# Small norm and routing arithmetic moved into PSUM banks, in a selective-scan mixer with a low-rank feed-forward layer

## The chip, the cores and the metric

The kernel runs on one core of one Trainium2 chip. The metric is the device time of one execution in microseconds. The engines are named as in the profile: PE is TensorE (PEld its weight loads), DVE is VectorE, ACT is ScalarE, POOL is GpSimd, SP is SyncE, which issues the DMAs.

## The reference, cut to what matters

There are four sequences of 512 tokens with 1024 features. Each goes through a mixer and a feed-forward layer, each followed by an addition and a layer norm.

```python
# mixer, D = 2048 channels, N = 16 states, R = 64
u, z = split(W_in @ x);  u = silu(causal_conv4(u) + conv_b)
dt, B, C = split(Wx @ u)                      # 64, 16, 16 rows
dt, B, C = rmsnorm(dt), rmsnorm(B), rmsnorm(C)  # eps 1e-6
delta = softplus(Wdt @ dt + dt_bias)
h_t = exp(delta_t * A) * h_{t-1} + delta_t * u_t * B_t
y_t = sum_n C_t[n] * h_t[n] + D * u_t
x1 = layernorm(x + W_out @ (y * silu(z)))     # eps 1e-5
# feed-forward: ranks 8, 16, 32, 64, the best one for each token
p = softmax(gate_w @ x1 + gate_b);  keep ranks up to the argmax, weight 1
out = layernorm(x1 + W @ x1 + b + B @ (mask * (A @ x1)))
```

## The kernel before, in words

The heart is the scan. For each of 4 sequences, 4 groups of 4 channel tiles and 16 states there is a unit, 256 in all. POOL forms the unit's input (`drive`, L1311, 128x2048), ACT forms four `decay` tiles in PSUM (L1146), DVE runs four scans (L913), PE transposes the states into two banks (`turn`, L771), and the products with C are added up in `y_acc`, either by DVE alone (`add`, L921) or by ACT and POOL (`scale` L1166, `sum` L1316). Everything else runs beside it: the products of the input projection for the next sequence (L798 to L800, three matmuls of split precision for each step), convolution and gates, the output projection (L821), the feed-forward products, the norms and the routing of the sequence before.

The order of each engine's work is fixed before launch. `Plan.arrange` simulates the five engines with a cost in microseconds and a due time for each piece (`put(engine, due, us, stage, key, needs, take, give, spare)`), and each engine then runs its list strictly in that order, waiting on semaphores. Pieces also take and give back buffers from pools: three PSUM banks (`bank`), four scratch tiles, four raw and four split weight slots. A product takes a bank only if another is free (`spare=1`). Five more banks hold the decays and the turned states.

The stages that the change touches:

- `ssm_mm`: dt, B and C for 4x128 tokens into one bank (96 columns each; the bank state_t0 for the first sequence). `ssm_copy` (ACT, L1210) copies it to `narrow` in SBUF and gives the bank back.
- `ssm_stat` (DVE): squares (L1037), three sums (L1042), three times scale and add epsilon (L1046). `ssm_sqrt` (ACT, L1213). `ssm_dt` (DVE, L1050, L1054): reciprocal, dt normalized, twice, into a scratch tile. `ssm_norm` (L1059, L1062, L1065): C and B normalized. `ssm_turn_dt` and `ssm_turn_b` (PE) transpose them. Then come delta, softplus, `du` and the drives of the next sequence.
- `route_rows` (PE) transposes the low-rank products and scores into a bank; `route_copy` (ACT, L1270) copies it to `narrow`. `route_max` (DVE, L1069, L1073, L1076), `route_exp` (ACT, L1280), `route_pick` (DVE, L1081 to L1103), `route_mask` (DVE, L1115), then `route_turn` (PE), `lora_cols`, `lora_low` and the products `f_lora`.
- Layer norms: statistics (L996, L1001) on DVE, `ln1_var` or `ln2_var` (DVE, L1009) adds epsilon, root on ACT (L1254), `ln_shift` (DVE, L1012, L1015), then `rows` are normalized on ACT (L1248), some in the last sequence on DVE (L1020).

## Time and profile before

| | |
|---|---|
| median of 3 runs | 2390.41 us (2381.63 to 2395.63) |
| profiled execution, its span | 2390.45 us, 2388.7 us |
| busy share PE, DVE, POOL, ACT | 89%, 87%, 75%, 63% |
| mean granted TensorE clock | 0.942 |
| chain that ended last, by engine | DVE 37%, PE 36%, issue 11%, ACT 6%, POOL 3% |
| one table load on ACT (L1146) | 1283 ns |

Busy time counts an instruction from its start to its end, whatever it does in between. The median of the runs and the profiled execution agree to 0.1 us; 1.75 us of the latter lie outside the span.

### The profile page before, as it was taken

Reading aid. Unit: us, or ns where it says so; the run is one execution under the profiler, and the core shown is the slowest. Engines: PE = TensorE matmul, PEld = TensorE weight load, DVE = VectorE, ACT = ScalarE, POOL = GpSimd, SP = SyncE. Lnnn points to the kernel's source line nnn. Section 1 sums busy time; section 2 is a strip of 40 time slices with the busy share of each in tenths; the row PEclk is TensorE's granted clock in tenths of the full one; section 3 lists DMA queues with packets and bytes.
Section 4 is the critical chain, followed back from the end, with each engine's and each line's share of the span. In section 5 each row is a group of like instructions: output and inputs, shape, how many; then the busy total and the mean of one; then the engine's idle time right before and its main releaser. Section 6 shows DMA issues by size and latency. Waiting matters only on the chain.

```text
span 2388.7 us, 30714 instructions
## 1 busy us (share of the span) xinstructions
PE 2124.3 (89%) x10528; PEld 1582.9 (66%) x10528; DVE 2084.7 (87%) x2464; ACT 1495.8 (63%) x2133; POOL 1803.3 (75%) x769
## 2 busy tenths in 40 slices
PE   8998679788879978889989998989989999898987
PEld 6767567676655547678866556767875567675556
DVE  4458899999999999989989998999979998999732
ACT  4388677776666575566667667575576568665421
POOL 4378888899699987868768996787768987688500
PEclk9989889899889989989989999999999999998998
DMA  4366566455323334566444334465453336353313
GB/s 149 131 220 216 183 208 201 162 199 174 99 73 91 111 116 152 180 219 202 151 151 125 112 95 144 139 239 170 148 184 104 108 100 208 102 168 117 85 50 132
DMA packets 152652, 353.53 MB, mean 148 GB/s; under 512 B 17776, under 2 KB 27376, under 8 KB 152496
## 3 DMA queue, kind: packets, MB, share of 16 engines
q1 hardware_dynamic: 152496, 351.56, 45.8%
q8 instruction: 84, 1.38, 0.2%
q14 instruction: 72, 0.59, 0.1%
HBM read 282.65 MB, written 68.85 MB: 147 GB/s over the span
## 4 chain that ended last, share of the span: by engine, by line
DVE 37%; PE 36%; issue 11%; ACT 6%; POOL 3%; DVEq 0%; ACTq 0%; POOLq 0%
DVE drive L913 20%; PE state_t L771 10%; DVE y_acc L921 9%; PE bank L821 7%; PE bank L798 5%; PE bank L799 5%; PE bank L800 5%; DVE scratch L928 2%; POOL drive L1311 2%; ACT decay L1146 1%; DVE ln_stats L996 1%; ACT L1146 1%; PE bank L771 1%; PE bank L866 1%; DVE rows L983 1%
## 5 line engine op out<-in xcount | busy, mean ns | idle before, releaser
L1311 POOL TENSOR_TENSOR drive<-delta_u,b_bcast 128x2048 f32<-128x2048 f32 x256 | 1171.3, 4577 | 142.9 <-PE state_t L771 140.6
L913 DVE TENSOR_TENSOR_SCAN drive<-decay,drive 128x512 f32<-128x512 f32 x1024 | 1193.2, 1203 | 74.3 <-ACT decay L1146 51.6
L1146 ACT ACTIVATE decay<-delta,a_sb 128x512 f32<-128x512 f32 x1024 | 693.6, 688 | 395.1 <-DVE drive L913 390.7
L771 PE MATMUL state_t<-identity,drive 128*128 128x128 f32 x4096 | 614.8, 291 | 183.5 <-DVE drive L913 138.2
L771 PEld LDWEIGHTS state_t<-identity,drive 128*128 128x128 f32 x4096 | 507.9, 149 | 394.0 <-DVE drive L913 197.7
L798 PE MATMUL bank<-cols_high,w_split 128*128 128x512 f32 (+1 forms) x1280 | 550.1, 430 | 15.9 <-POOL w_split L1336 8.4
L921 DVE SCALAR_TENSOR_TENSOR y_acc<-state_t,c_rows,y_acc 128x512 f32<-128x512 f32 x711 | 505.4, 734 | 51.4 <-PE state_t L771 49.6
L800 PE MATMUL bank<-cols_high,w_split 128*128 128x512 f32 (+1 forms) x1280 | 513.5, 401 | 0.0
L799 PE MATMUL bank<-cols_low,w_split 128*128 128x512 f32 (+1 forms) x1280 | 513.1, 401 | 0.0
L821 PE MATMUL bank<-channels,w_raw 128*128 128x512 f32 x960 | 452.3, 595 | 0.0
L1316 POOL TENSOR_TENSOR y_acc<-y_acc,scaled 128x512 f32<-128x512 f32 x249 | 320.4, 1287 | 170.7 <-ACT scaled L1166 167.6
L798 PEld LDWEIGHTS bank<-cols_high,w_split 128*128 128x128 f32 (+1 forms) x1280 | 248.7, 194 | 61.9 <-issue 10.7
L800 PEld LDWEIGHTS bank<-cols_high,w_split 128*128 128x128 f32 (+1 forms) x1280 | 246.7, 193 | 58.2 <-issue 0.2
L799 PEld LDWEIGHTS bank<-cols_low,w_split 128*128 128x128 f32 (+1 forms) x1280 | 248.9, 194 | 40.6 <-issue 0.5
L821 PEld LDWEIGHTS bank<-channels,w_raw 128*128 128x128 f32 x960 | 166.0, 192 | 122.7 <-issue 121.1
L1166 ACT ACTIVATE scaled<-state_t,c_rows 128x512 f32<-128x512 f32 x249 | 170.1, 683 | 117.8 <-PE state_t L771 91.3
L1336 POOL TENSOR_TENSOR w_split<-w_raw,w_split 128x512 fp32r<-128x512 f32 (+1 forms) x114 | 145.9, 1288 | 84.1 <-ACT w_split L1186 84.0
L928 DVE SCALAR_TENSOR_TENSOR scratch<-bank,conv_w_sb,scratch 128x511 f32<-128x511 f32 (+2 forms) x192 | 142.6, 743 | 36.9 <-ACT scratch L1192 32.4
L1146 ACT ACT_TABLE_LOAD x91 | 116.8, 1283 | 1.6
L1325 POOL TENSOR_TENSOR delta_u<-delta,channels 128x512 f32<-128x512 f32 x64 | 80.6, 1286 | 35.3 <-ACT delta L1235 15.4
L1201 ACT ACT_TABLE_LOAD x63 | 80.8, 1283 | 40.6 <-PE bank L800 39.7
L1332 POOL TENSOR_TENSOR channels<-channels,scratch 128x512 f32<-128x512 f32 x64 | 82.5, 1305 | 24.0 <-DVE channels L973 20.8
(152 smaller groups left out, 1397.6 us busy)
## 6 DMA issues: line engine op xcount, KB each, us to landing
w_split<-w_split SPq DMA_DIRECT2D x288, 512.0 KB, 3.6
b_bcast<-b_rows SPq DMA_DIRECT2D x256, 256.0 KB, 3.4
w_raw<-in_w_out SPq DMA_DIRECT2D x128, 256.0 KB, 2.9
w_raw<-in_w_in SPq DMA_DIRECT2D x96, 256.0 KB, 4.1
gates<-scratch SPq DMA_DIRECT2D x64, 256.0 KB, 3.8
scratch<-gates SPq DMA_DIRECT2D x64, 256.0 KB, 4.5
rows<-in_x_rows SPq DMA_DIRECT2D x4, 2048.0 KB, 9.5
out<-rows SPq DMA_DIRECT2D x16, 512.0 KB, 5.1
```

The costliest lines, as they stand in the source:

```text
L771: last = engine.transpose(bank[0:tile.shape[1], i * P:(i + 1) * P], tile, identity[:, :])
L798: engine.matmul(bank[:, :], high[:, k % WK, :], cols_high[:, k, :], start=first, stop=False)
L799: engine.matmul(bank[:, :], high[:, k % WK, :], cols_low[:, k, :], start=False, stop=False)
L800: engine.matmul(bank[:, :], low[:, k % WK, :], cols_high[:, k, :], start=False, stop=last).then_inc(signal[stage])
L821: engine.matmul(bank[:, :], tile[:, k % WK, :], chan[s % 2][:, k, :], start=(k == tiles[0]), stop=(k == tiles[-1])).then_inc(signal["o_mm"])
L913: engine.tensor_tensor_scan(state, decay[(GT * s + t) % DECAYS][:, :], state, 0.0, ALU.mult, ALU.add).then_inc(signal["scan"])
L921: engine.scalar_tensor_tensor(y_acc[:, tt, :], bank[:, :], c, y_acc[:, tt, :], ALU.mult, ALU.add).then_inc(signal["add"])
L928: m = engine.scalar_tensor_tensor(conv[:, back:T], bank[:, 0:T - back], conv_w[:, j, KC - 1 - back:KC - back], conv[:, back:T], ALU.mult, ...
L1146: engine.activation(decay[i % DECAYS][:, :], delta[:, g % 2, t, :], ACT.Exp, scale=a_sb[:, j, n:n + 1]).then_inc(signal["decay"])
L1166: engine.activation(scaled[:, :], bank[:, :], ACT.Copy, scale=c_rows[b % 2][:, tt, n:n + 1]).then_inc(signal["scale"])
L1311: engine.tensor_tensor(drive[key % DRIVES][:, :, :], du[:, :, :], row, ALU.mult).then_inc(signal["drive"])
L1316: engine.tensor_tensor(y_acc[:, tt, :], y_acc[:, tt, :], scaled[:, :], ALU.add).then_inc(signal["sum"])
```

## The change: what it does

- `narrow`, `score` and `prob` in SBUF go. dt, B, C and the normalized C before its weight stay in the bank of `ssm_mm`; low-rank rows, scores, probabilities and an inverse stay in the bank of `route_rows`. B normalized goes to a small SBUF tile `b_narrow`. Of the two tensors that a DVE instruction reads there, at most one now lies in SBUF.
- `ssm_copy` and `route_copy` go. Squares are formed on ACT out of the bank (`ssm_square`). Scale and epsilon of the mixer's norms, and epsilon of the layer norms, become scale and bias of the root on ACT; the bias is an SBUF column set once at the start. `ssm_sqrt` is two instructions. `ln1_var` and `ln2_var` go, their waits move to `ln1_sqrt` and `ln2_sqrt`.
- The bank of `ssm_mm` is given back after `ssm_norm` in place of `ssm_copy`, that of `route_rows` after `route_mask` in place of `route_copy`. The first `turn` waits for `ssm_norm`.
- The costs given to the planner are smaller: `ssm_stat` 2.2 to 0.7, `ssm_dt` 1.2 to 0.9, `ssm_norm` 1.0 to 0.5, `route_max` 1.6 to 0.6, `route_pick` 3.5 to 2.2, `route_mask` 2.4 to 1.3. So the order of all work is computed anew.

```diff
-        put("ACT", due + 0.4, 0.5, "ssm_copy", b, [...], give=[("bank", ("ssm_mm", b))] if b else [])
-        put("DVE", due + 0.5, 2.2, "ssm_stat", b, [("ssm_copy", b)], take=[("scratch", ("twice", b))])
+        put("ACT", due + 0.4, 0.5, "ssm_square", b, [("ssm_mm", (b, TT - 1))], take=[("scratch", ("twice", b))])
+        put("DVE", due + 0.5, 0.7, "ssm_stat", b, [("ssm_square", b)])
...
+        put("DVE", due + 0.7, 0.5, "ssm_norm", b, [("ssm_dt", b)] + ([("ssm_turn_b", b - 1)] if b else []),
+            give=[("bank", ("ssm_mm", b))] if b else [])
...
-        put("ACT", due + 1, 0.45, "route_copy", s, [...], give=[("bank", ("route_rows", s))])
-        put("DVE", due + 1.2, 1.6, "route_max", s, [("route_copy", s)])
+        put("DVE", due + 1.2, 0.6, "route_max", s, [("route_rows", s)])
         put("ACT", due + 1.3, 0.3, "route_exp", s, [("route_max", s)])
-        put("DVE", due + 1.4, 3.5, "route_pick", s, [("route_exp", s)])
-        put("DVE", due + 1.5, 2.4, "route_mask", s, [("route_pick", s)], take=[("scratch", ("mask", s))])
+        put("DVE", due + 1.4, 2.2, "route_pick", s, [("route_exp", s)])
+        put("DVE", due + 1.5, 1.3, "route_mask", s, [("route_pick", s)], take=[("scratch", ("mask", s))], give=[("bank", ("route_rows", s))])
...
+        def ssm_rows(b):
+            bank = banks[place["bank", ("ssm_mm", b)]] if b else state_banks[0]
+            return bank[:, 0:TT * S].rearrange("p (a s) -> p a s", a=TT), bank[:, TT * S:TT * (S + N)].rearrange("p (a s) -> p a s", a=TT)
+        def route_bank(s):
+            bank, at = banks[place["bank", ("route_rows", s)]], TT * C
+            score, prob = (bank[:, at + i * TT * NR:at + (i + 1) * TT * NR].rearrange("p (a r) -> p a r", a=TT) for i in range(2))
+            return bank[:, 0:at].rearrange("p (a c) -> p a c", a=TT), score, prob, bank[:, at + 2 * TT * NR:at + (2 * NR + 1) * TT]
...
-                    engine.tensor_scalar(ln_rstd[:, :], ln_mv[:, :, 1], LN_EPS, None, ALU.add).then_inc(signal[stage])
...
-                    engine.tensor_tensor(squares, narrow[:, :, :], narrow[:, :, :], ALU.mult).then_inc(vector_chain)
...
-                    for i, (a, z) in enumerate(segments):
-                        m = engine.tensor_scalar(ssm_rstd[:, i, :], ssm_rstd[:, i, :], 1.0 / (z - a), MIXER_EPS, ALU.mult, ALU.add)
...
-                    engine.tensor_tensor(c, narrow[:, :, R + N:S], ssm_rstd[:, 2, :].unsqueeze(2).broadcast_to([P, TT, N]),
+                    engine.tensor_tensor(c_normed, src[:, :, R + N:S], ssm_rstd[:, 2, :].unsqueeze(2).broadcast_to([P, TT, N]),
...
-                    engine.tensor_tensor(score[:, :, :], narrow[:, :, R:R + NR], gate_b[:, :].unsqueeze(1).broadcast_to([P, TT, NR]),
+                    engine.tensor_tensor(score, rows_r[:, :, R:R + NR], gate_b[:, :].unsqueeze(1).broadcast_to([P, TT, NR]),
...
+                    engine.activation(by_rank(("twice", key))[:, :, 0:S], ssm_rows(key)[0], ACT.Square).then_inc(signal["ssm_square"])
...
-                    engine.activation(ssm_rstd[:, :, :], ssm_rstd[:, :, :], ACT.Sqrt).then_inc(signal["ssm_sqrt"])
+                    engine.activation(ssm_rstd[:, 0, :], ssm_rstd[:, 0, :], ACT.Sqrt, bias=mixer_eps[:, :], scale=1.0 / R)
+                    engine.activation(ssm_rstd[:, 1:3, :], ssm_rstd[:, 1:3, :], ACT.Sqrt, bias=mixer_eps[:, :],
+                                      scale=1.0 / N).then_inc(signal["ssm_sqrt"])
...
-                    engine.activation(ln_rstd[:, :], ln_rstd[:, :], ACT.Sqrt).then_inc(signal[stage])
+                    engine.activation(ln_rstd[:, :], ln_mv[:, :, 1], ACT.Sqrt, bias=ln_eps[:, :]).then_inc(signal[stage])
```

## Rows read from the trace of the kernel before

**Rows 1.** Busy time of the engines in three stretches, clock and DMA last.
```profile
core 0: us, PE busy (x) PEld busy (x) DVE busy (x) ACT busy (x) POOL busy (x), PEclk, DMA share, GB/s
720.00:860.00 140.00, 137.80 (x604) 80.47 (x603) 138.98 (x155) 81.59 (x124) 132.20 (x53) 1.00 0.35 98
860.00:1020.00 160.00, 125.67 (x656) 98.89 (x655) 153.94 (x187) 101.06 (x149) 128.86 (x62) 0.89 0.50 161
1720.00:1860.00 140.00, 127.64 (x623) 90.09 (x622) 119.01 (x135) 98.63 (x131) 106.22 (x41) 0.96 0.46 143
```

**Rows 2.** Groups by form on DVE: busy us, mean ns, idle before.
```profile
L1009 DVE TENSOR_SCALAR ln_rstd<-ln_mv 128x4 f32<-128x4 f32 x8 | 15.4, 1926 | 0.1
...
L1046 DVE TENSOR_SCALAR ssm_rstd<-ssm_rstd 128x4 f32<-128x4 f32 x12 | 11.8, 1044 | 0.1
...
L1103 DVE TENSOR_TENSOR keep<-keep,score 128x4 f32<-128x4 f32 x12 | 9.6, 796 | 0.4
...
L1037 DVE TENSOR_TENSOR scratch<-narrow 128x384 f32<-128x384 f32 x4 | 7.2, 1803 | 3.1 <-ACT narrow L1210 3.1
...
L1069 DVE TENSOR_TENSOR score<-narrow,gate_b_sb 128x16 f32<-128x16 f32 x4 | 6.8, 1706 | 5.8 <-ACT narrow L1270 5.8
...
L1059 DVE TENSOR_TENSOR c_rows<-narrow,ssm_rstd 128x64 f32<-128x64 f32 x4 | 6.2, 1550 | 0.0
...
L1087 DVE TENSOR_TENSOR prob<-prob,row_stat 128x16 f32<-128x16 f32 x4 | 4.1, 1026 | 0.1
...
L1076 DVE TENSOR_TENSOR score<-score,row_stat 128x16 f32<-128x16 f32 x4 | 3.2, 795 | 0.1
```

**Rows 3.** Single lines: duration ns shortest/median/longest, first and last start us.
```profile
L1009 DVE TENSOR_SCALAR ln_rstd<-ln_mv x8: 143/170/9797, 875.9 to 2379.5; 128x4 f32<-128x4 f32 x8
...
L1046 DVE TENSOR_SCALAR ssm_rstd<-ssm_rstd x12: 156/282/4505, 116.4 to 1727.2; 128x4 f32<-128x4 f32 x12
...
L1103 DVE TENSOR_TENSOR keep<-keep,score x12: 167/168/4511, 919.6 to 2327.4; 128x4 f32<-128x4 f32 x12
...
L1059 DVE TENSOR_TENSOR c_rows<-narrow,ssm_rstd x4: 214/796/4397, 119.4 to 1739.7; 128x64 f32<-128x64 f32 x4
...
L1037 DVE TENSOR_TENSOR scratch<-narrow x4: 555/1124/4410, 115.1 to 1725.3; 128x384 f32<-128x384 f32 x4
```

**Rows 4.** Order of time on DVE and POOL at two places: start us, us.
```profile
1491.27 4.18 DVE L1069 TENSOR_TENSOR score<-narrow,gate_b_sb 128x16 f32<-128x16 f32 x1
...
1490.82 4.60 POOL L1311 TENSOR_TENSOR drive<-delta_u,b_bcast 128x2048 f32<-128x2048 f32 x1
...
998.06 9.80 DVE L1009 TENSOR_SCALAR ln_rstd<-ln_mv 128x4 f32<-128x4 f32 x1
...
1003.32 4.51 POOL L1311 TENSOR_TENSOR drive<-delta_u,b_bcast 128x2048 f32<-128x2048 f32 x1
```

**Rows 5.** Single lines with one operand in PSUM, and with both in SBUF.
```profile
L921 DVE SCALAR_TENSOR_TENSOR y_acc<-state_t,c_rows,y_acc x711: 702/737/753, 159.6 to 2252.3; 128x512 f32<-128x512 f32 x178
...
L1030 DVE TENSOR_TENSOR cols_low<-bank,cols_high x27: 661/677/693, 892.4 to 2316.5; 128x512 fp32r<-128x512 f32 x27
...
L1026 DVE TENSOR_TENSOR cols_low<-drive,cols_high x8: 683/693/693, 4.3 to 19.6; 128x512 fp32r<-128x512 f32 x8
...
L1015 DVE SCALAR_TENSOR_TENSOR ln_shift<-ln_mv,ln_rstd x8: 161/164/1298, 883.2 to 2380.2; 128x4 f32<-128x4 f32 x8
```

**Rows 6.** Groups by form on ACT, without and with a bias in SBUF.
```profile
L1243 ACT ACTIVATE scratch<-bank 128x512 f32<-128x512 f32 x40 | 23.7, 592 | 28.3 <-PE bank L821 27.9
...
L1243 ACT ACTIVATE scratch<-bank,ffn_b_sb 128x512 f32<-128x512 f32 x28 | 19.0, 681 | 24.7 <-PE bank L807 24.6
```

**Rows 7.** Order of time in the second sequence's projections' norm.
```profile
617.97 0.47 ACT L1210 ACTIVATE narrow<-bank 128x384 f32<-128x384 f32 x1
...
634.84 0.21 DVE L1065 TENSOR_TENSOR c_rows<-c_rows,c_ln_w_sb 128x64 f32<-128x64 f32 x1
```

**Rows 8.** Chain that ended last, pieces in order of time, first and last of nine.
```profile
619.53 4.34 DVE scratch L1037
...
2052.57 1.98 DVE score L1069
```

More of the change, by code:

```diff
@@ L781, in _ @@
                     if i == 0:
-                        e.wait_ge(*done("ssm_copy", 0))
+                        e.wait_ge(*done("ssm_norm", 0))
                     if i >= TURNED:
@@ L875, in _ @@
                     e.wait_ge(*done("ssm_norm", key))
-                    turned(bank, [narrow[:, tt, R:R + N] for tt in range(TT)]).then_inc(signal[stage])
+                    turned(bank, [b_narrow[:, tt, :] for tt in range(TT)]).then_inc(signal[stage])
                 elif stage == "x1_turn":
@@ L1201, in _ @@
                     engine.activation(gate[:, :], banks[place["bank", ("g_mm", key)]][:, :], ACT.Silu).then_inc(signal["g_silu"])
-                elif stage == "ssm_copy":
+                elif stage == "ssm_square":
+                    if before["scratch", ("twice", key)] is not None:
+                        e.wait_ge(*done(*before["scratch", ("twice", key)]))
                     e.wait_ge(*done("ssm_mm", (key, TT - 1)))
-                    if key > 1:
-                        e.wait_ge(*done("route_mask", key - 2))
-                    if key:
-                        e.wait_ge(*done("ssm_turn_b", key - 1))
-                    bank = banks[place["bank", ("ssm_mm", key)]] if key else state_banks[0]
-                    src = bank[:, 0:TT * S].rearrange("p (a s) -> p a s", a=TT)
-                    engine.activation(narrow[:, :, :], src, ACT.Copy).then_inc(signal["ssm_copy"])
+                    engine.activation(by_rank(("twice", key))[:, :, 0:S], ssm_rows(key)[0], ACT.Square).then_inc(signal["ssm_square"])
                 elif stage == "ssm_sqrt":
                     e.wait_ge(*done("ssm_stat", key))
-                    engine.activation(ssm_rstd[:, :, :], ssm_rstd[:, :, :], ACT.Sqrt).then_inc(signal["ssm_sqrt"])
+                    e.wait_ge(eps_set, 2)
+                    engine.activation(ssm_rstd[:, 0, :], ssm_rstd[:, 0, :], ACT.Sqrt, bias=mixer_eps[:, :], scale=1.0 / R)
+                    engine.activation(ssm_rstd[:, 1:3, :], ssm_rstd[:, 1:3, :], ACT.Sqrt, bias=mixer_eps[:, :],
+                                      scale=1.0 / N).then_inc(signal["ssm_sqrt"])
                 elif stage == "dt_cols":
@@ L1263, in _ @@
                     engine.activation(cols_high[:, h, :], banks[place["bank", ("x1_turn", key)]][:, :], ACT.Copy).then_inc(signal["x1_high"])
-                elif stage == "route_copy":
-                    e.wait_ge(*done("route_rows", key))
-                    e.wait_ge(*done("ssm_turn_b", min(key + 1, NSEQ - 1)))
-                    if key == NSEQ - 1:
-                        e.wait_ge(*done("route_mask", key - 1))
-                    src = banks[place["bank", ("route_rows", key)]][:, 0:TT * C].rearrange("p (a c) -> p a c", a=TT)
-                    engine.activation(narrow[:, :, 0:C], src, ACT.Copy).then_inc(signal["route_copy"])
                 elif stage == "route_lift":
```

86 lines of the change are left out of this document (38 added, 48 removed).

## Prediction

> **What bounds the kernel now.** I read the page first, then the stretches, the groups of instructions by form, single instructions, the chain of waits, and the order of time around the changed stages. The page's busy shares (DVE 87%, PE 89%) do not say which engine sets the pace, so take the stretches. Between 720 and 860 us nothing of the changed code runs: DVE is busy 138.98 of 140 us and POOL 132.20. From 860 to 1020 us, where a norm, the routing and another norm fall, DVE is busy 153.94 of 160 us, but POOL only 128.86, PE 125.67, and the granted TensorE clock falls from 1.00 to 0.89. From 1720 to 1860 us, with a projections' norm, DVE has 21 us of idle time and PE 12 [rows 1]. So DVE is the bound or next to it nearly everywhere, and in the changed stages it is busy while the others starve.
>
> What it is busy with is odd. Eight groups of tiny instructions take 64.3 us in total [rows 2]. The cheapest instance of L1009 takes 0.143 us and its dearest 9.797; L1103 spreads from 0.167 to 4.511 and L1037 from 0.555 to 4.410 [rows 3]. The order of time says what the long ones do. L1069, 16 elements, starts at 1491.27 and takes 4.18 us, to 1495.45; POOL's drive began at 1490.82 and took 4.60, to 1495.42. L1009 starts at 998.06 and ends at 1007.86; POOL's queue was full all that time, and its next drive ended at 1003.32 + 4.51 = 1007.83 [rows 4]. The narrow instruction stands until POOL leaves a gap; that is waiting recorded as busy time.
>
> Which instructions suffer? Those with two SBUF tensors, and the one-input tensor_scalar. Not those with one tensor in PSUM and one in SBUF: L921 ran 711 times next to a POOL that is busy three quarters of the span, and its longest took 0.753 us; L1030 never passed 0.693 [rows 5].
>
> **The change, part by part.**
>
> *Waits removed.* Busy time less the count times the free duration, which is near the cheapest instance (L1009 0.143, L1046 0.156, L1103 0.167, L1059 0.214, L1037 0.555; the 16-element ones as L1103). L1009: 15.4 - 8 x 0.16 = 14.1. L1046: 11.8 - 12 x 0.18 = 9.6. L1103: 9.6 - 12 x 0.17 = 7.6. L1069: 6.8 - 4 x 0.17 = 6.1. L1059: 6.2 - 4 x 0.21 = 5.4. L1037: 7.2 - 4 x 0.56 = 5.0. L1087: 3.4. L1076: 2.5. Sum 53.7 us of DVE [rows 2, 3]. L1009, L1046 and L1037 disappear; the others get one PSUM operand. I take their waits as gone because of L921 and L1030; that a PSUM-to-PSUM form such as L1059's new one waits isn't excluded by a row, and its term is 5.4.
>
> *A wait that comes back.* L1015 keeps two SBUF operands (ln_mv, ln_rstd). It met POOL idle in most of its eight cases, its longest 1.298 [rows 5], because L1009 had just drained POOL. With L1009 gone it is the first in its stage to meet POOL. Lower bound nothing; upper bound L1009's own mean, 14.1 / 8 = 1.8 us each, 14 us. I take 4, nearer the low end, as L1015 comes after the ScalarE root, at another phase. Remaining: 49.7.
>
> *Work removed and added on DVE.* L1037 4 x 0.56, L1046 12 x 0.18, L1009 8 x 0.16: 5.7 us less [rows 2, 3]. The PSUM operands: at 512 columns the median of cols_low from SBUF is 0.693, and that with PSUM 0.677 [rows 5], so nothing by the rows. I count 25 instructions a sequence that get a PSUM operand (two for dt, three for B and C, three in route_max, nine in route_pick, eight in route_mask), 100 in all. Bound: 0 to 0.06 each, 6 us (the latter is the whole spread of the nearest forms, 0.753 - 0.693); I take 1. Net 4.7 less.
>
> The Trainium skill (VectorE: DVE Perf Modes, section on the TRN2 errata) speaks against the change: a PSUM source has a fixed part of 120 cycles where an SBUF source has 58, at 0.96 GHz 65 ns more for each instruction. An estimate by that page puts 6.5 us back on DVE in place of my 1, and the forecast some 4 us later. This trace has no narrow instruction with a PSUM operand, so it can only contradict the page at 512 columns.
>
> *ScalarE.* route_copy goes (four copies), ssm_square takes the place of ssm_copy, ssm_sqrt becomes two instructions, and 16 roots get a bias in SBUF. A bias costs 0.681 - 0.592 = 0.09 us [rows 6]: 1.4 us. All in all within 1 us of nothing, on an engine that is busy 63% of the span. If Square needed a table of its own, each switch would be a table load; a bias or copy has none beside it in the trace, and the bound is two loads a sequence, eight of 1.283 us (the table of the profile above), 10 us of ScalarE time under cover of its idle time; I take nothing. New on ScalarE is the wait of ssm_square for the scratch slot, which the DVE had; decays stand behind it, and scans behind these. The order gives the slot only when free, so I take nothing. The other way round, the root of the layer norms no longer waits for L1009 with the decays of the next scans queued behind it.
>
> *Banks.* This is the price. ssm_mm's bank was free when the copy ended (617.97 + 0.47 = 618.4) and is now kept until c_rows are done, which in this trace is at 635.05 [rows 7]. Six such stretches, three of ssm and three of the routing beside the scans, would be 12 to 17 us long. Only three banks circulate, and a product asks for one with a spare beside it: while one is kept, products go one at a time. A product is 8 steps of some 0.7 us, 5.5 us on PE, and then its bank waits for ScalarE and DVE. Without the removed waits (up to 8 us in each) the stretches shrink to about 8 us, so PE loses perhaps one half-product in each: bounds 0 and 6 x 5.5 = 33 us of PE; I take 6 x 1.5 = 9 us, of which DVE's bound hides half: 4 us. Nothing is moved on SP's or POOL's queue by hand, but the order is worked out again from new costs and times of release, and interleaves loads and scans differently everywhere behind the first norm. I cannot price that from rows: its sign is open, and I take 0 with a margin of 8 us either way.
>
> *From DVE time to the end.* 49.7 + 4.7 = 54.4 us of DVE. How much reaches the end? The chain of waits runs through the narrow instructions: nine pieces of over 1.9 us, the first L1037 at 619.53, the largest L1009 with 9.80 us [rows 4], the last L1069 at 2052.57, 41 us together [rows 8]. That is three quarters of the waits. Each wait also stops PE and lets its clock fall, which is given back. Against it: when a wait goes, POOL, which ran ahead in it, is next; in the undisturbed stretch it is at 132 of 140 us. I pass on 80%: 43.5 us. Less 4 for banks: 39.5. The profiled execution took 2390.45 us with a span of 2388.7, and the median of the runs is 2390.41, so no correction: 2351 us.
>
> In the tail the routing and both norms run beside an idle POOL, every one of them at its cheapest. There I expect under 2 us.
>
> **Rivals.**
> *The waits turn into others (0.22).* POOL or PE comes next at once: only the removed instructions and 40% of the waits pass: 0.4 x 54.4 = 22, 2390 - 22 + 2 for banks = 2370. For it: PE 137.80 and POOL 132.20 in 140 us [rows 1]. Against: both idle in just the stretches concerned.
> *All of it passes, and more (0.15).* DVE's 54.4, and with the clock back up PE never falls behind: 2390 - 54 - 8 for a luckier order = 2328.
> *Nothing to be measured (0.09).* The waits stay since a PSUM operand doesn't keep a narrow DVE instruction clear of POOL: only 5.7 - 1 us remain, 2386. Against it stand 711 rows of L921. Or gain and bank price cancel.
> *Slower, by the banks (0.05).* If products stop for the whole of each keeping, six times about 15 us, 88 us less the waits removed from them, 46 us or so are lost on PE, and its clock falls after each, some 2 us apiece: 2390 - 44 + 58 = 2404. It decides from the point where PE loses over 44 us in them, more than the stretches hold without the waits, so the order must turn bad as well.
>
> **The numbers.** The forecast, 2351, has 0.49, by itself 2338 to 2362. With 0.22 at 2370 and 0.15 at 2328 the range that leaves out 2 in 10 is 2326 to 2376. Within 0.5% is 2378.5 to 2402.4, about what a measurement can tell from no change. Faster: 0.49 + 0.22 + 0.15 = 0.86; same 0.09; slower 0.05.
>
> **What would show it.** Right: L1069, L1087, L1076, L1059, L1103 at 0.17 to 0.3 us with no instance over 0.5; no TENSOR_SCALAR on ln_rstd or ssm_rstd; DVE's busy time down by 45 us or more; ScalarE's waits on L1009 and L1046 gone; clock in 860 to 1020 above 0.92. Banks: idle PE in front of the first product after ssm_mm, released by c_rows. Wrong would be: narrow instructions of PSUM operands with long instances; L1015 with instances of 4 us; or PE, POOL with idle time in the same total as before, then the order costs what the waits gave.

## The result, and the profile after

The changed kernel takes 2355.91 us, the median of 4 runs (2353.31 to 2363.13), against 2392.04 for the kernel before beside it: ratio 0.9863, 95% interval 0.983 to 0.9895. A second measurement with the same text gave 2354.54 (2352.99 to 2355.08), ratio 0.9848 (0.9834 to 0.9861). The forecast was 2351, so the time came out 3.5 to 4.9 us later than said, within the likeliest case's own range of 2338 to 2362. The profiled execution of the first measurement is its slowest run, 2363.13 us with a span of 2361.3; that of the second has 2351.2. Both are used below, and the text says which.

The page of the changed kernel, first execution: engines, share of the span, instructions, then TensorE's granted clock.

```profile
span 2361.3 us, 30676 instructions
...
PE 2112.9 (89%) x10528; PEld 1569.5 (66%) x10528; DVE 2032.5 (86%) x2440; ACT 1493.5 (63%) x2132; POOL 1805.6 (76%) x771
```

The page of the second execution:

```profile
span 2351.2 us, 30676 instructions
...
PE 2112.1 (90%) x10528; PEld 1569.8 (67%) x10528; DVE 2021.4 (86%) x2440; ACT 1494.6 (64%) x2132; POOL 1805.2 (77%) x771
```

The page of before had DVE at 2084.7 us, PE at 2124.3 and ACT at 1495.8. So DVE is busy 52.2 us less in the first execution and 63.3 less in the second, while the span fell by 27.4 and 37.5.

The groups by form on DVE and ACT after the change (busy us, mean ns, idle before) answer to [rows 2]:

```profile
L1016 DVE SCALAR_TENSOR_TENSOR ln_shift<-ln_mv,ln_rstd 128x4 f32<-128x4 f32 x8 | 14.2, 1772 | 0.3
...
L1253 ACT ACTIVATE ln_rstd<-ln_mv,ln_eps 128x4 f32<-128x4 f32 x8 | 2.4, 297 | 10.4 <-DVE ln_mv L1010 10.3
...
L1097 DVE TENSOR_TENSOR keep<-keep,bank 128x4 f32<-128x4 f32 x12 | 1.9, 162 | 0.4
...
L1081 DVE TENSOR_TENSOR bank<-bank,row_stat 128x16 f32<-128x16 f32 x4 | 0.7, 183 | 0.1
L1070 DVE TENSOR_TENSOR bank<-bank,row_stat 128x16 f32<-128x16 f32 x4 | 0.7, 182 | 0.1
...
L1063 DVE TENSOR_TENSOR bank<-bank,gate_b_sb 128x16 f32<-128x16 f32 x4 | 0.7, 170 | 5.8 <-PE bank L894 5.8
...
L1051 DVE TENSOR_TENSOR bank<-bank,ssm_rstd 128x64 f32<-128x64 f32 x3 | 0.6, 215 | 0.0
```

L1097 is the former L1103, L1063 the former L1069, L1070 L1076, L1081 L1087, and L1051 with L1059 the former L1059 and its neighbour. The eight groups of [rows 2] held 64.3 us; what is left of them is under 5 us. In their place one group stands out, `ln_shift`.

Single lines of the changed kernel, first execution (shortest, median, longest in ns), which answer to [rows 3] and [rows 5]:

```profile
L1016 DVE SCALAR_TENSOR_TENSOR ln_shift<-ln_mv,ln_rstd x8: 163/164/10966, 867.9 to 2352.3; 128x4 f32<-128x4 f32 x8
...
L1097 DVE TENSOR_TENSOR keep<-keep,bank x12: 161/161/164, 895.8 to 2298.5; 128x4 f32<-128x4 f32 x12
...
L1063 DVE TENSOR_TENSOR bank<-bank,gate_b_sb x4: 157/170/183, 893.4 to 2295.9; 128x16 f32<-128x16 f32 x4
...
L1059 DVE TENSOR_TENSOR c_rows<-bank,c_ln_w_sb x3: 215/217/218, 621.1 to 1705.0; 128x64 f32<-128x64 f32 x3
```

In L1097, L1063 and L1059 shortest and longest now differ by 3 to 26 ns, where the former L1103 and L1059 differed by a factor of 20 and more. One instance of L1016 took 10.97 us. The order of time on DVE and POOL around it:

```profile
979.91 0.17 DVE L1013 RECIPROCAL ln_rstd<-ln_rstd 128x4 f32<-128x4 f32 x1
980.11 10.97 DVE L1016 SCALAR_TENSOR_TENSOR ln_shift<-ln_mv,ln_rstd 128x4 f32<-128x4 f32 x1
991.00 1.21 DVE L922 TENSOR_TENSOR_SCAN drive<-decay,drive 128x512 f32<-128x512 f32 x1
...
979.42 2.57 POOL L1333 TENSOR_TENSOR cols_low<-w_raw,cols_high 128x512 fp32r<-128x512 f32 x2
981.90 9.16 POOL L1303 TENSOR_TENSOR drive<-delta_u,b_bcast 128x2048 f32<-128x2048 f32 x2
```

POOL ran four instructions back to back until 981.90 + 9.16 = 991.06, and the four elements of `ln_shift` stood until 991.08. The chain that ended last has this piece as `980.11 10.98 DVE ln_shift L1016`, its longest. In the second execution the same line, in the same order of work:

```profile
L1016 DVE SCALAR_TENSOR_TENSOR ln_shift<-ln_mv,ln_rstd x8: 162/164/1259, 868.0 to 2342.2; 128x4 f32<-128x4 f32 x8
```

The instance in question, and POOL beside it, in the second execution:

```profile
980.00 0.17 DVE L1013 RECIPROCAL ln_rstd<-ln_rstd 128x4 f32<-128x4 f32 x1
980.20 0.62 DVE L1016 SCALAR_TENSOR_TENSOR ln_shift<-ln_mv,ln_rstd 128x4 f32<-128x4 f32 x1
...
979.50 2.54 POOL L1333 TENSOR_TENSOR cols_low<-w_raw,cols_high 128x512 fp32r<-128x512 f32 x2
981.99 4.65 POOL L1303 TENSOR_TENSOR drive<-delta_u,b_bcast 128x2048 f32<-128x2048 f32 x1
```

All of it lies 0.08 to 0.09 us later and is otherwise the same. There the instruction ended at 980.82, at the seam between POOL's two `cols_low` (979.50 + 2.54 / 2 = 980.77, taking the two as equally long). In the first execution it arrived as early before that seam and did not get through, nor at the next two. The wait differs by 10.97 - 0.62 = 10.35 us, and the spans by 10.1: one narrow instruction, caught or not at a seam of POOL, moved the whole kernel.

The stretches of [rows 1] after the change, second execution:

```profile
720.00:860.00 140.00, 134.79 (x592) 79.09 (x591) 138.68 (x160) 83.43 (x126) 134.81 (x55) 0.99 0.41 114
860.00:1020.00 160.00, 136.44 (x724) 110.63 (x725) 148.47 (x197) 110.13 (x163) 129.79 (x63) 0.92 0.56 191
1720.00:1860.00 140.00, 135.16 (x637) 87.77 (x636) 132.35 (x146) 95.94 (x135) 125.34 (x49) 1.00 0.45 134
```

From 860 to 1020 us PE does 136.44 us of work where it did 125.67, with 0.92 of its clock where it had 0.89 (above 0.92 had been expected; the first execution, with the long wait in it, has 0.89). The third stretch holds other work than before, since all runs earlier.

So far the change did what it says. What is missing shows only in the last stretch, from the start of the last scan to the end. Before, and then after (second execution), columns as in [rows 1]:

```profile
2247.80:2388.70 140.90, 118.01 (x497) 79.95 (x495) 45.07 (x94) 29.25 (x45) 7.49 (x6) 0.92 0.28 88
```

```profile
2196.60:2351.20 154.60, 131.42 (x536) 86.79 (x534) 47.04 (x95) 31.06 (x47) 8.18 (x7) 0.93 0.27 85
```

The last scan starts 51.2 us earlier, but what follows it is 13.7 us longer, and PE has 13.4 us more to do there: 536 matmuls in place of 497. Products that ran beside the scans before now run after them, where nothing hides them. 51.2 - 13.7 = 37.5, the difference of the spans. (The 39 matmuls are 27 of the output projection, L828, formerly L821, and 12 transposes of its results.)

### The profile page after: what moved, and what is told of

Its sections match the earlier page's. It is cut to its first block, busy times and chain, and to the rows that moved or that the text cites. A ratio compares the mean times of both kernels' runs of the same rounds, so it can differ in the third digit from the quotient of the medians.

```text
span 2361.3 us, 30676 instructions
## 1 busy us (share of the span) xinstructions
PE 2112.9 (89%) x10528; PEld 1569.5 (66%) x10528; DVE 2032.5 (86%) x2440; ACT 1493.5 (63%) x2132; POOL 1805.6 (76%) x771
## 4 chain that ended last, share of the span: by engine, by line
PE 42%; DVE 31%; issue 10%; ACT 6%; POOL 4%; DVEq 0%; ACTq 0%; POOLq 0%
DVE drive L922 17%; PE state_t L778 11%; PE bank L828 11%; DVE y_acc L930 7%; PE bank L805 5%; PE bank L807 5%; PE bank L806 5%; DVE scratch L937 2%; POOL drive L1303 2%; PE bank L778 2%; ACT L1140 1%; ACT decay L1140 1%; DVE ln_stats L1005 1%; ACT rows L1241 1%; PE decay L828 1%
## 5 line engine op out<-in xcount | busy, mean ns | idle before, releaser
L778 PEld LDWEIGHTS state_t<-identity,drive 128*128 128x128 f32 x4096 | 501.2, 148 | 369.1 <-DVE drive L922 173.8
L930 DVE SCALAR_TENSOR_TENSOR y_acc<-state_t,c_rows,y_acc 128x512 f32<-128x512 f32 x709 | 504.8, 734 | 60.0 <-PE state_t L778 56.2
L805 PE MATMUL bank<-cols_high,w_split 128*128 128x512 f32 (+1 forms) x1272 | 542.2, 426 | 13.4 <-POOL w_split L1328 8.2
L807 PE MATMUL bank<-cols_high,w_split 128*128 128x512 f32 (+1 forms) x1272 | 507.8, 399 | 0.0
L806 PE MATMUL bank<-cols_low,w_split 128*128 128x512 f32 (+1 forms) x1272 | 506.1, 398 | 0.0
L828 PE MATMUL bank<-channels,w_raw 128*128 128x512 f32 x944 | 445.0, 597 | 1.3 <-POOL channels L1324 1.3
L805 PEld LDWEIGHTS bank<-cols_high,w_split 128*128 128x128 f32 (+1 forms) x1272 | 245.0, 193 | 60.8 <-issue 6.5
L807 PEld LDWEIGHTS bank<-cols_high,w_split 128*128 128x128 f32 (+1 forms) x1272 | 242.6, 191 | 56.8 <-issue 0.4
L828 PEld LDWEIGHTS bank<-channels,w_raw 128*128 128x128 f32 x944 | 164.2, 192 | 125.3 <-issue 124.8
L1317 POOL TENSOR_TENSOR delta_u<-delta,channels 128x512 f32<-128x512 f32 x64 | 80.6, 1285 | 11.8 <-ACT delta L1228 10.0
```

The lines of the kernel that those rows point to most:

```text
L778: last = engine.transpose(bank[0:tile.shape[1], i * P:(i + 1) * P], tile, identity[:, :])
L805: engine.matmul(bank[:, :], high[:, k % WK, :], cols_high[:, k, :], start=first, stop=False)
L806: engine.matmul(bank[:, :], high[:, k % WK, :], cols_low[:, k, :], start=False, stop=False)
L807: engine.matmul(bank[:, :], low[:, k % WK, :], cols_high[:, k, :], start=False, stop=last).then_inc(signal[stage])
L828: engine.matmul(bank[:, :], tile[:, k % WK, :], chan[s % 2][:, k, :], start=(k == tiles[0]), stop=(k == tiles[-1])).then_inc(signal["o_mm"])
L930: engine.scalar_tensor_tensor(y_acc[:, tt, :], bank[:, :], c, y_acc[:, tt, :], ALU.mult, ALU.add).then_inc(signal["add"])
```

## The experiments

Three sets of kernels were run, and one kernel by itself, each with 5 rounds beside the kernel before (2390.82, 2391.71, 2392.54 and 2390.44 us). "After" below is the second measurement, 2354.54 us, ratio 0.9848. It was the first kernel of the first set:

> The changed kernel once more, beside the others of this set. Every theory: 2356 us, ratio 0.983 to 0.989 to the kernel before. It is the measure for the next three.

Measured: 2354.54 us, as told above.

**The new order with the old operands.** The order of work is that of the changed kernel; the instructions are those of before.

```diff
-                    engine.activation(by_rank(("twice", key))[:, :, 0:S], ssm_rows(key)[0], ACT.Square).then_inc(signal["ssm_square"])
+                    engine.activation(narrow[:, :, :], ssm_rows(key)[0], ACT.Copy).then_inc(signal["ssm_square"])
...
+                    engine.tensor_tensor(squares, narrow[:, :, :], narrow[:, :, :], ALU.mult).then_inc(vector_chain)
...
+                    engine.tensor_copy(narrow[:, :, 0:C], banks[place["bank", ("route_rows", key)]][:, 0:TT * C].rearrange("p (a c) -> p a c", a=TT))
...
+                    engine.tensor_scalar(ln_rstd[:, :], ln_mv[:, :, 1], LN_EPS, None, ALU.add).then_inc(signal[stage])
```

The copy of the routing rows runs on DVE, at the head of `route_max`, and the epsilon of the layer norms right behind the last statistics, since the new order has no places for them.

> The changed kernel's plan, so the same order of work and the same times at which the banks are given back, but the narrow arithmetic with its operands in SBUF as before (copy to SBUF on ScalarE in place of the squares; the routing's copy on VectorE, since the order has no place for it on ScalarE, 4 x 0.4 us; epsilons on VectorE). Theory A, the waits of VectorE on GpSimd are what the time came from: the waits return, some 40 to 60 us of busy time on VectorE, and the time is 2380 to 2395 us, ratio 0.995 to 1.0. Rival B, the new order of work brought the gain: it stays at 2352 to 2362, ratio 0.985 to 0.988. In between, shares are read off in proportion.

Measured: 2416.4 us (2411.31 to 2423.27), ratio 1.0114 (1.0096 to 1.0132). Groups by form of this kernel:

```profile
L1051 DVE TENSOR_TENSOR scratch<-narrow 128x384 f32<-128x384 f32 x4 | 13.9, 3474 | 3.1 <-ACT narrow L1226 3.1
L1121 DVE TENSOR_TENSOR keep<-keep,score 128x4 f32<-128x4 f32 x12 | 8.3, 690 | 0.4
L1023 DVE TENSOR_SCALAR ln_rstd<-ln_mv 128x4 f32<-128x4 f32 x8 | 7.4, 926 | 1.3 <-DVE ln_mv L1013 1.2
L1116 DVE TENSOR_TENSOR score<-prob,row_stat 128x16 f32<-128x16 f32 x4 | 6.2, 1543 | 0.0
```

The waits are back, in part on other members of the group than in [rows 2]: the squares have 13.9 us where they had 7.2. DVE's busy time came out as theory A said, the time itself 21 us above its range. With one and the same order the new operands take 2078.4 - 2021.4 = 57.0 us off DVE and 2416.4 - 2354.5 = 61.9 us off the time (spans 63.4). Next to the kernel before, this one costs 2416.4 - 2390.8 = 25.6 us, for the new order, with the banks that are kept in it and the routing's copy on DVE. DVE's waits in sum are not the reason, as DVE is busy 6.3 us less than before (2078.4 against 2084.7). Its last scan starts at 2259.40, 11.6 us later than before, and what follows it takes 155.2 us, 14.3 more than before.

**Banks kept.** The kernel before, which only gives its banks back later.

```diff
-            [("route_mask", b - 2)] if b > 1 else []), give=[("bank", ("ssm_mm", b))] if b else [])
+            [("route_mask", b - 2)] if b > 1 else []))
...
-        put("DVE", due + 0.7, 1.0, "ssm_norm", b, [("ssm_dt", b)])
+        put("DVE", due + 0.7, 1.0, "ssm_norm", b, [("ssm_dt", b)], give=[("bank", ("ssm_mm", b))] if b else [])
...
-            give=[("bank", ("route_rows", s))])
...
-        put("DVE", due + 1.5, 2.4, "route_mask", s, [("route_pick", s)], take=[("scratch", ("mask", s))])
+        put("DVE", due + 1.5, 2.4, "route_mask", s, [("route_pick", s)], take=[("scratch", ("mask", s))], give=[("bank", ("route_rows", s))])
```

> The kernel before, with the one edit that the banks of the projections and of the routing rows are given back after the norm and the mask as in the changed kernel (and so an order computed anew). Theory A, the bank price is small (forecast 4 us, bound 33): 2390 to 2400 us, ratio 1.0 to 1.004. Rival C, keeping the banks is dear and the changed kernel would have gained much more without it: 2410 us or more, ratio over 1.008.

Measured: 2398.32 us (2398.01 to 2401.79), ratio 1.0035 (1.0023 to 1.0048), 7.5 us by the medians. The stretch behind its last scan:

```profile
2242.20:2396.50 154.30, 131.49 (x536) 86.85 (x534) 47.31 (x97) 31.21 (x48) 8.19 (x7) 0.93 0.27 85
```

The same 536 matmuls and the same 13.4 us more as in the changed kernel. The banks alone push those products behind the last scan. The last scan itself comes 5.6 us earlier than before (2242.2 against 2247.8), presumably since the products that were put off no longer stand between it and its inputs; 154.3 - 140.9 - 5.6 is the 7.8 us by which the span grew.

**`ln_shift` without its wait.** In all sequences but the last the negated product of mean and root is formed on ACT, column by column; the order is that of the changed kernel.

```diff
-                    engine.scalar_tensor_tensor(ln_shift[:, :], ln_mv[:, :, 0], -1.0, ln_rstd[:, :],
+                    engine.scalar_tensor_tensor(ln_shift[:, :], ln_mv[:, :, 0], -1.0, ln_rstd[:, 0:TT],
...
+                        for a in range(TT):
+                            m = engine.activation(ln_shift[:, a:a + 1], ln_mv[:, a, 0:1], ACT.Copy, scale=ln_rstd[:, TT + a:TT + a + 1])
...
+                        m = engine.activation(ln_rstd[:, TT:2 * TT], ln_rstd[:, 0:TT], ACT.Copy, scale=-1.0)
```

> The changed kernel, same order, with the one narrow VectorE instruction that still reads two SBUF tensors (ln_shift, 14.2 us busy, longest 10.97) replaced in sequences 0 to 2: the negated root on ScalarE, one reciprocal over eight columns on VectorE, four one-column products on ScalarE ahead of the rows. Theory A, the returned wait costs the end nearly its length: 12 us less on VectorE, some 9 less at the end, 2344 to 2350, and 0.993 to 0.997 of the changed kernel. Rival D, a wait is hidden or the next one takes its place: 2353 to 2359, no difference from the changed kernel; 1 to 2 us more on ScalarE in each norm would then show as a loss.

Measured: 2358.28 us (2357.41 to 2359.45), ratio 0.9865 (0.9851 to 0.9878), 4 us above the changed kernel of the same set; the intervals of the ratios overlap a little, the times of the runs don't (2352.99 to 2355.08 there). No gain, as rival D said: in the profiled execution of that set the instruction had cost 3.8 us of DVE, not 14.2, and 24 instructions of 0.282 us and 6 of 0.205 us on ACT replaced it. The long wait of the first execution is no steady loss of this order of work.

**The old costs in the planner.** The changed kernel with the six costs of before.

```diff
-        put("DVE", due + 0.5, 0.7, "ssm_stat", b, [("ssm_square", b)])
+        put("DVE", due + 0.5, 2.2, "ssm_stat", b, [("ssm_square", b)])
...
-        put("DVE", due + 1.4, 2.2, "route_pick", s, [("route_exp", s)])
+        put("DVE", due + 1.4, 3.5, "route_pick", s, [("route_exp", s)])
```

> The changed kernel with the planner's six costs as they were before (2.2, 1.2, 1.0, 1.6, 3.5, 2.4), operands and bank times as changed. Theory E, the smaller costs matter since the work order now fits the shorter chains: 2362 to 2372 us, ratio 0.988 to 0.992. Rival F, they are of no account beside the waits: 2351 to 2358, ratio 0.983 to 0.986.

Measured: 2360.35 us (2354.4 to 2362.28), ratio 0.9869 (0.9846 to 0.9892). The new costs are worth 5 us by the ratios, at the edge of what the intervals tell apart, and between the two theories. In this kernel's profile `ln_shift` has 9.4 us, with one instance of 7.3, where the second execution of the changed kernel has 3.8, so the 5 us can be this wait as well as the costs.

**The new costs with the old operands.** The kernel before with the six new costs, which are too small for it.

```diff
-        put("DVE", due + 0.5, 2.2, "ssm_stat", b, [("ssm_copy", b)], take=[("scratch", ("twice", b))])
+        put("DVE", due + 0.5, 0.7, "ssm_stat", b, [("ssm_copy", b)], take=[("scratch", ("twice", b))])
```

> The kernel before with the six new costs alone, banks given back as before. The kernel with the new order and the old operands lost 25 us; keeping the banks alone lost 7.5. Theory E: the plan is now too hopeful for chains with waits in them and loses the rest, 2400 to 2412 us, ratio 1.004 to 1.009. Rival F: 2388 to 2394, ratio 0.999 to 1.002, and the 25 us belong to where the waits happened to fall.

Measured: 2386.55 us (2382.12 to 2391.42), ratio 0.9982 (0.997 to 0.9993). A gain of 4 us by the ratio, 5 by the medians, outside both expected ranges: costs that are wrong for the old instructions don't by themselves make the 25.6 us. The costs together with the kept banks were not run.

**Only the epsilons on ScalarE.** The kernel before, in its own order; L1009 and L1046 are gone, the roots have scale and bias, everything else is as it was.

```diff
-                    engine.tensor_scalar(ln_rstd[:, :], ln_mv[:, :, 1], LN_EPS, None, ALU.add)
...
-                        m = engine.tensor_scalar(ssm_rstd[:, i, :], ssm_rstd[:, i, :], 1.0 / (z - a), MIXER_EPS, ALU.mult, ALU.add)
...
-                    engine.activation(ln_rstd[:, :], ln_rstd[:, :], ACT.Sqrt)
+                    engine.activation(ln_rstd[:, :], ln_mv[:, :, 1], ACT.Sqrt, bias=ln_eps[:, :])
```

> The kernel before, its order unchanged, with only the epsilons (and the mixer norms' scale) moved into the root on ScalarE: L1009 and L1046 go, 27.2 us busy in the profile of before, 23.7 of it waits. Theory A, with the order the same a removed wait passes to the end nearly whole, as 57 us of VectorE's time passed as 62 between the changed kernel and its old operands: 20 us gained, 2368 to 2374, ratio 0.990 to 0.993. Rival D, the next narrow instruction with two SBUF operands (squares, shift, C) inherits half of it or more: 2378 to 2385, ratio 0.995 to 0.998, and busy time of those goes up.

Measured: 2364.82 us (2363.77 to 2368.76), ratio 0.9895 (0.9876 to 0.9914), 27 us off by the medians. The page and one line of this kernel:

```profile
PE 2113.1 (89%) x10528; PEld 1571.1 (66%) x10528; DVE 2068.7 (87%) x2446; ACT 1497.7 (63%) x2137; POOL 1803.3 (76%) x769
```

```profile
L1012 DVE SCALAR_TENSOR_TENSOR ln_shift<-ln_mv,ln_rstd x8: 161/164/5658, 877.7 to 2358.1; 128x4 f32<-128x4 f32 x8
```

`ln_shift` inherits part of the wait: 11.8 us in its eight instances where it had 3.5. Of the 27.2 us in L1009 and L1046 DVE is therefore rid of only 16.0. Yet the span of this execution, the slowest of the five, is 22.1 us below that of before, and the median time 27. The last scan starts at 2225.70, 22.1 us earlier, and the 140.9 us behind it are those of before: in its own order, and with the banks given back early, nothing is put off: 497 matmuls again.

**The routing as before, in the changed kernel.** `route_copy`, `score`, `prob`, the old costs and the early return of that bank are back; the rest is the changed kernel.

```diff
-        put("DVE", due + 1.2, 0.6, "route_max", s, [("route_rows", s)])
+        put("ACT", due + 1, 0.45, "route_copy", s, [("route_rows", s), *other],
+            give=[("bank", ("route_rows", s))])
+        put("DVE", due + 1.2, 1.6, "route_max", s, [("route_copy", s)])
```

> The changed kernel with the routing part undone: rows copied to SBUF on ScalarE, bank given back after the copy, scores and probabilities in SBUF, old costs of the routing pieces. The mixer norms and layer norms stay as changed. Moving the epsilons alone gained 27 us of the 36. Theory H, the remaining 9 are the sum of waits gained and banks and order lost in either part, and the routing part, with 22 us of waits gone and a bank kept for about 13 us three times, is a clear gain: this kernel is 8 to 16 us behind the changed one, 2363 to 2372. Rival I, the routing part's bank takes back what its waits give: 2351 to 2360.

Measured: 2366.45 us (2359.1 to 2369.35), ratio 0.9883 (0.9866 to 0.99): the routing part is worth 8 us by the ratios and 10 by the medians. Behind the last scan this kernel needs 2364.7 - 2218.4 = 146.3 us, 8.3 less than the changed kernel, so its scans end some 22 us later. The order behind the scans depends on more than this bank, though: with the old costs in the changed kernel it takes 159.6 us (2358.5 - 2198.9), and with the new costs in the kernel before 146.3 (2386.7 - 2240.4). Not all of the difference need be the routing's: in this profile `ln_shift` has 9.4 us, 5.6 more than in the second execution of the changed kernel.

**The mixer's norms as before, in the changed kernel.** `ssm_copy`, the squares on DVE and `narrow` are back, the epsilons stay on ACT.

```diff
-        put("ACT", due + 0.4, 0.5, "ssm_square", b, [("ssm_mm", (b, TT - 1))], take=[("scratch", ("twice", b))])
-        put("DVE", due + 0.5, 0.7, "ssm_stat", b, [("ssm_square", b)])
+        put("ACT", due + 0.4, 0.5, "ssm_copy", b, [("ssm_mm", (b, TT - 1))] + ([("ssm_turn_b", b - 1)] if b else []), give=[("bank", ("ssm_mm", b))] if b else [])
+        put("DVE", due + 0.5, 2.2, "ssm_stat", b, [("ssm_copy", b)], take=[("scratch", ("twice", b))])
```

> The changed kernel with the mixer norms' operand part undone: projections copied to SBUF, squares on VectorE, bank given back after the copy, old costs of these pieces; epsilons stay on ScalarE, layer norms and routing as changed. Theory H: the mixer part removes 12 to 13 us of waits (L1037, L1059, L1054) and keeps its bank where ssm_mm has kept it 17 us already: 0 to 5 us behind the changed kernel, 2355 to 2361. Rival J, the mixer's bank is the dear one, PE cannot start the next products beside it: this kernel is ahead, 2340 to 2352.

Measured: 2365.33 us (2358.54 to 2367.36), ratio 0.9878 (0.9862 to 0.9895): this part is worth 7 us by the ratios and 9 by the medians, more than had been expected of it. The stretches behind the last scan, first of this kernel, which keeps only the routing's bank, then of the one above, which keeps only the mixer's:

```profile
2209.20:2363.50 154.30, 131.65 (x536) 86.98 (x534) 47.07 (x95) 31.09 (x47) 8.23 (x7) 0.93 0.28 86
```

```profile
2218.40:2364.70 146.30, 123.03 (x512) 81.98 (x510) 46.05 (x94) 29.30 (x45) 7.05 (x6) 0.94 0.28 87
```

Over all kernels of this section the split is clean: PE has 536 matmuls or more behind the last scan (551 with the old costs) wherever the routing's bank is kept until `route_mask`, and 497 to 512 wherever it is given back after the copy. So the products are put off by the routing's bank, and hardly by the mixer's.

**`dt_rest` on GpSimd.** The changed kernel has further instructions with two SBUF tensors beside a busy POOL. One is L963, eight times, 64x256 (another, L1027, has one instance of 3.67 us and is left as it is). It is moved to POOL itself, where it can't wait for POOL.

```diff
-        put("POOL" if pool == "split" else "DVE", due - 3, 0.23 + part if pool == "split" else 0.35, rest, w, [("w_high", w)], give=[("raw", w)])
+        put("POOL", due - 3, 0.23 + part if pool == "split" else 0.75, rest, w, [("w_high", w)], give=[("raw", w)])
```

> The changed kernel with dt_rest (64x256, two SBUF operands, 8 instances, all in the first sequence, 9.6 us busy of which 6.2 waits) on GpSimd in place of VectorE, with waits on its neighbours there. Theory A: 4 to 8 us less than the changed kernel, 2347 to 2351. Rival G: GpSimd is as busy as VectorE in the first sequence (235 of 260 us between 140 and 400) and eight instructions more there, or another order, take it back: 2353 to 2362.

Measured: 2339.25 us (2336.75 to 2343.49), ratio 0.9787 (0.9764 to 0.9809). It beats both kernels, the changed one by 15 us, more than either theory gave, and that with 10.9 us in `ln_shift`. What L963 did in the changed kernel (order of time, second execution, DVE and then PE):

```profile
394.97 5.40 DVE L963 TENSOR_TENSOR dt_slot<-w_raw,dt_slot 64x256 fp32r<-64x256 f32 x1
...
402.33 0.90 PE L778 MATMUL state_t<-identity,drive 128*128 128x128 f32 x3 [4.15 <-DVE y_acc L930]
```

PE's last product before it ended at 402.33 - 4.15 = 398.18, 3.2 us after the wait began, and PE stood until 402.33. In its place, in the new kernel:

```profile
L1331 POOL TENSOR_TENSOR dt_slot<-w_raw,dt_slot 64x256 fp32r<-64x256 f32 x8 | 5.9, 733 | 7.7 <-ACT dt_slot L1174 7.3
```

**`dt_rest` on GpSimd, in the kernel before.** The same edit.

> The kernel before with dt_rest alone moved to GpSimd. On the changed kernel this move gained 16 us, with waits of 6.2 us to remove. Theory A, waits in the first sequence cost more than their length and the gain is of the move: 10 to 18 us here too, 2373 to 2382. Rival K, most of the 16 us was a luckier order: here 0 to 6 us, 2385 to 2392, or a loss.

Measured: 2370.64 us (2368.28 to 2377.84), ratio 0.9909 (0.9891 to 0.9926), 22 us off. So the gain is not one of the changed kernel alone; as the order is made anew here too, this doesn't yet say how much of it is the waits.

**`dt_rest` on GpSimd, with the order kept.** The plan is made as if it ran on DVE; the eight pieces then change lists.

```diff
     plan.arrange()
+    plan.work["POOL"] = sorted(plan.work["POOL"] + [w for w in plan.work["DVE"] if w[1] == "dt_rest"], key=lambda w: w[0])
+    plan.work["DVE"] = [w for w in plan.work["DVE"] if w[1] != "dt_rest"]
```

> The changed kernel with the eight dt_rest subtractions on GpSimd again, but with the order of the changed kernel kept on every engine: the plan is made as if they ran on VectorE, and they are then taken out of VectorE's list and put into GpSimd's at their planned start. In the earlier run, where the plan was made anew for GpSimd, the same move gained about 16 us though the waits that it removes were 8 us of VectorE's busy time.
>
> Theory L, the waits do it (a VectorE that stands also stops TensorE, and TensorE's clock falls): with the order kept the gain is nearly the same, 10 to 18 us below the changed kernel's 2355, so 2337 to 2345 us, ratio 0.977 to 0.981. The granted clock from 360 to 480 us should be near 0.99 as in that run.
>
> Theory M, the newly made order does it: with the order kept only the waits themselves can be gained, less the interruption of GpSimd, 0 to 8 us, so 2347 to 2355 us, ratio 0.982 to 0.985. VectorE's busy time should then fall by 7 to 8 us without TensorE's clock in 360 to 480 rising.

Measured: 2348.61 us (2346.12 to 2349.86), ratio 0.9823 (0.9809 to 0.9836), 6 us below the changed kernel by both. The stretch from 360 to 480 us in the changed kernel, in this one, and with the order made anew:

```profile
360.00:480.00 120.00, 101.80 (x528) 81.46 (x527) 115.88 (x128) 86.65 (x125) 110.13 (x51) 0.93 0.56 180
```

```profile
360.00:480.00 120.00, 105.98 (x564) 84.35 (x563) 114.71 (x132) 92.43 (x133) 116.38 (x56) 0.96 0.59 194
```

```profile
360.00:480.00 120.00, 107.17 (x573) 85.23 (x571) 114.55 (x131) 93.77 (x135) 116.88 (x56) 0.99 0.63 203
```

The time is theory M's, though the clock rose halfway, which M had excluded. So of the 15 us some 6 are the waits, and 9 the order that the planner made once it saw these pieces on POOL. DVE is busy 9.9 us less here (2011.5 against 2021.4) and the span 6.9 us shorter. Of the 9.7 us that L963 had in the changed kernel 8 x 0.42 = 3.4 were work and 6.3 waits, and POOL is busy 5.0 us more instead.

## Why the forecast came out nearly right, point by point

**What the waits are.** Right. Once its operands were moved no narrow instruction waited; those that read two SBUF tensors did, wherever they were left (L1016, L963, and most of the group again in the old operands with the new order), and so did the one-input TENSOR_SCALAR. PSUM to PSUM forms, whose term was left open (the former L1059, 5.4 us), took 0.206 to 0.223 us. Only "stands until POOL leaves a gap" is too strict: in the second execution a seam between two POOL instructions was enough.

**Waits removed, 53.7 us, and base work, 5.7.** Right in size: the eight groups went from 64.3 us to under 5.

**The PSUM operand, 1 us taken, 6 at most.** It is nothing: 0.162 us against 0.167 for four elements, 0.157 to 0.183 against 0.174 for 16, 0.206 to 0.223 against 0.214 for 64. The 65 ns for each instruction that the Trainium skill (VectorE: DVE Perf Modes, section on the TRN2 errata) would add are not there, so these rows contradict the page for such small tiles; the 6.5 us by that page are not in the time either.

**The wait that comes back, 4 us taken, 0 to 14.** The second profiled execution has nearly none: 3.8 us in L1016 in all, where L1015 had had 3.5. The first has 14.2, near the upper bound, and with it an instance over 4 us, which the prediction had named as a sign of being wrong. With the epsilons alone moved it inherits 8.3 us, and with the old costs, with the routing as before and with `dt_rest` on GpSimd it has 9.4, 9.4 and 10.9 us. The bounds were right, and the term isn't a number but a spread, between orders of work and between executions of one kernel: 10.35 us of wait stood beside 10.1 us of span.

**DVE down by 54.4 us.** It is down by 52.2 and 63.3. The second is above the forecast for the wait that didn't come back, and for waits outside the eight groups (L1054, now L1046, went from 5.2 to 3.1 us).

**ScalarE, nothing.** Right: 1495.8 us before, 1494.6 after. The roots take 0.297 and 0.285 us, Square costs no table load of its own (before L1200 there is none, and the loads in all number 200 in place of 203). ScalarE's wait for the epsilon on DVE (23.2 us in the kernel before) became one of 10.3 us for the statistics.

**80% of DVE's time reaches the end, 43.5 us.** This step failed, and upward. With the order fixed, 57.0 us of DVE gave 61.9 us of time, 109% in place of 80; the epsilons alone, 16.0 of DVE for 22.1 of span. Behind a wait PE runs dry and goes on with a lower clock: between the two kernels of one order PE itself is busy 2129.1 - 2112.1 = 17.0 us less for the same 10528 matmuls, at a mean granted clock of 0.949 in place of 0.935. That this is the reason for more than 100% is argued, not taken apart. Nor is more than 100% of DVE's time a rule: L963 moved with the order kept gave 6.9 us of span for 9.9 of DVE, though POOL took on its work there. The argument from POOL, that it would be next, didn't hold.

**Banks, 4 us, and the reordering, 0 with 8 either way.** This step failed too, downward. Banks and order together cost 25.6 us with the old operands; what they cost with the new ones can't be read off by itself. In the changed kernel 13.7 us more stand in one place, behind the last scan, and banks kept longer, the routing's above all, are enough to put them there. That is not yet the price: in the kernel that only keeps its banks the same stretch grew by 13.4 us, the scans ended 5.6 earlier, and the time rose by 7.5, nearly twice the 4 that had been taken. The prediction looked for the price beside the kept banks, as idle PE in front of the next product. There is hardly any: in the second sequence's norm ScalarE has read the bank at 615.31 and `c_rows` are done at 621.30, so it is held 6.0 us longer and not the 16.6 that the old kernel's waits made of this stretch, and PE stood 0.20 and 0.30 us. A product that finds no bank isn't a gap on PE there and then, since turns of the scan fill it; by the matmuls behind the scans it is put off until these are over. "In the tail I expect under 2 us" was right for the norms and the routing in it and overlooked this. What stays open is the rest of the new order: with the old operands its last scan comes 11.6 us later than before. The costs alone don't make it (they gave 4 us); the copy of the routing rows on DVE in that experiment accounts for 4 x 0.43 = 1.7 us. Whether the remainder is where the waits now fall (the squares have 6.7 us more) or the order itself was not taken apart.

So 39.5 us net was forecast as 43.5 - 4, and 36 to 37.5 came as 62 - 25.6, if the two are taken one after the other (all new operands in the old order were not run). The mechanism of the waits was right, and the closeness of the sum is luck: two errors of some 20 us cancel.

**The rivals.** "The waits turn into others" (2370) and "nothing" are out: with the order fixed all the operands together passed on more than they took off DVE. Only with the epsilons alone did 10.5 of 27.2 us turn into other waits. "All of it passes" (2328) was right that all of it passes, and wrong in counting the new order as a gain of 8 us. "Slower, by the banks" had the right cause of the loss with the wrong place and, at 58 us, twice the size.

**The parts.** The epsilons give 25 to 27 us (put into the kernel before), the routing's operands 8 to 10 and the mixer's 7 to 9 (taken out of the changed kernel). Together that is 40 to 46 against 36, so they overlap, and each kernel has an order of its own in it; the epsilons alone left 8.3 us of their waits to `ln_shift` and 2.2 to the normalized dt (5.2 to 7.4 us in its eight instructions), which also read two SBUF tensors.

## What to carry to other kernels

Look for tiny instructions whose shortest and longest instance differ by a factor of ten, and see what the other engine does at both ends: time in them is waiting, and taking it away can gain more than the busy time says (61.9 us for 57.0 here, though 6.9 for 9.9 where the work went to POOL), as the engines behind it are idle and slow afterwards. Price a buffer that is held longer not at its place but at the end of the phase: work without a deadline is put off until nothing hides it, so count the matmuls behind the last scan before and after. And with an order that is planned anew, run the new instructions in the old order or the old ones in the new, otherwise two large terms of opposite sign look like one small one.

## What the runs showed of the hardware

- A DVE instruction with two SBUF tensors waited not only for the POOL instruction that was running, but through four that followed each other without a gap, up to 10.97 us for 4 elements. The Trainium skill (SBUF — State Buffer, section "Who interferes with whom") says that such an instruction contends with a GpSimd instruction that reads SBUF, and that one with at most one SBUF input doesn't, outside the two-port performance modes. For TENSOR_TENSOR and SCALAR_TENSOR_TENSOR these traces agree in both: 709 instances of L930, with one operand in PSUM, had 0.754 us as their longest.
- The same wait came or didn't come, 10.97 or 0.62 us, in two executions in which the instructions around it stood within 0.01 us of the same positions to each other. The profile counts it as busy time.
- RECIPROCAL and the reductions, with one SBUF tensor, never waited in the same stages (L1013 0.17 us right in front of the 10.97), though the TENSOR_SCALAR forms L1009 and L1046 of the kernel before, which also have one, did (up to 9.80 and 4.51 us). Why they did, no run here shows.
- An activation of 128x16 within PSUM took 0.153 us where that from SBUF to SBUF took 0.212. The page "ScalarE: Activation LUTs" of the Trainium skill, in "Step-by-step: what each stage is for", calls PSUM the faster destination; the rows agree, though both of the operands moved here.
